# Difference attention's first round: which engine makes two low weight parts, and where two ternary means are summed

## The chip, the cores and the metric

The kernel runs on one core of one Trainium2 chip. The metric is the time of one execution on the device, in microseconds (us); lower is better. The core has five engines that run their own instruction streams and wait for each other through semaphores: TensorE (PE), VectorE (DVE), ScalarE (ACT), GpSimd (POOL) and SyncE (SP, which only issues transfers here).

## The reference

Two layers work on 8 x 64 tokens of width 512. Each is a cross attention, a self attention and a feed-forward block, each with a residual sum. The change lies in layer 0's self attention ("difference attention"), which computes, for 16 heads of width 128 split into two halves:

```python
x = layernorm(x)
q, k, v = x @ Wq, x @ Wk, x @ Wv                    # 512 x 2048 each
a1 = softmax(q[..., :64] @ k[..., :64].T / 8 + causal)
a2 = softmax(q[..., 64:] @ k[..., 64:].T / 8 + causal)
x = x + ((a1 - sigmoid(lambda_init) * a2) @ v) @ Wo
```

(The listing is a shortened form; the names are the reference's.) Beside it the kernel prepares the weights of the feed-forward block that follows. That block's weights are made ternary in groups of 64:

```python
scale = clip(mean(abs(w_g)), 1e-8)
w_hat = clip(round(w_g / scale), -1, 1) * scale
```

## The kernel before, in words

**Numbers.** Products of float32 are made of three fast matmuls (`mm3`, L41 to L43): every operand is split into a high part (rounded to the fp32r type) and a low part (the rest). Weights come by DMA into one of four buffers `w_raw` of 128 x 1024. ScalarE writes the high part (`split_high`, L153); the low part, raw minus high, is written either by GpSimd (`split_low`, L157) or by VectorE (`low`, L1689). Buffer 0 holds a piece of Wq, 1 of Wk, 2 of Wv, 3 of Wo. A buffer is refilled when its low part is done: `fill` waits on `split_lo[k]` in SP's queue.

**Rounds.** `DiffAttention` goes over `PAIRS` = 8 rounds `i`, two heads in each. In a round TensorE makes queries and keys, the scores (L1813), the values, then transposes the probabilities (L1836), multiplies them with the values (L1844), and one round later multiplies the result with W_o in `project(i - 1)`, which sums in PSUM banks 4 to 7 from round 1 to the end. ScalarE copies what TensorE leaves in banks 0 to 3 out of PSUM. VectorE does the softmax.

**The norm ahead of it.** The residual's last two 128-token tiles (m = 2, 3) are added by VectorE (L1207), their statistics taken (L193), the variance prepared (L262, a 128 x 2 operation), ScalarE takes the root (L267), VectorE normalises (`da_xn`, L275), TensorE transposes (L292), ScalarE writes the high part (`da_xT_high`, L286) and VectorE the low part (L280). The first two tiles went the same way some 7 us earlier.

**Ternary steps.** `TernaryWeights` has 24 steps `s` of 1024 columns, three to a round. A step is a load (`tw_raw`), on ScalarE a cast (`scalar_cast`, L2012), absolute values (L2016), signs (L2020) and a copy of the means out of PSUM (`scalar_wide`, L2024), on TensorE two matmuls that make the means (L2060), and on VectorE six operations (`vector_quantise`, L2040 to L2051). In every round steps 3i+2, 3i+3 and 3i+4 put their means in banks 0 and 1, which the values used before, one step after the other: each waits until the banks have been read.

**Order.** All queues are written out by hand. GpSimd's: `split_low(0)`, `split_low(2)` (`gpsimd_first`), then the end of the window attention, two memsets of `da_a` (L1553), a wait for the four tiles of `da_xn`, `split_low(1)`, `split_low(3)`. SP's, after the window attention: the mask, lambda, then `load(1, 0)`, `load(1, 1)`, `load(1, 2)` (L149), the ternary loads of steps 4 and 5 (L1997), `load(2, 0)`, step 6, `load(2, 1)`, `load(2, 2)`, `load(1, 3)`, steps 7 and 8, and so on. VectorE's in round 0: step 0's quantising, three small operations on lambda, `low(0)` for round 1, step 1's quantising, the softmax, `low(1)` and `low(2)` for round 1, step 2's quantising; from round 1 on `low(3)` stands at the end of a round.

Of the kernel before, what the change touches and what calls it, by code (L numbers as in the profile page):

```python
# [23 lines left out]
M = N // P  # L24
# [8 lines left out]
PAIRS = H // 2  # L33
# [139 lines left out]
class LayerNorm:  # L173
# [44 lines left out]
    def scalar(self, act):  # L218
        self.scalar_std(act)
        self.scalar_turned(act)  # L220
# [75 lines left out]
class ContextSums:  # L296
# [62 lines left out]
    def gpsimd(self, pool):  # L359
        nc = self.c.nc  # L360
        nc.gpsimd.memset(self.ones8[:, :], 1.0).then_inc(self.memsets, 1)
        nc.gpsimd.memset(self.col[:, :, 1], 1.0 / T).then_inc(self.memsets, 1)
        nc.gpsimd.memset(self.col[:, :, 2:32], 0.0).then_inc(self.memsets, 1)
# [1109 lines left out]
class DiffAttention:  # L1473
# [67 lines left out]
            if i < PAIRS - 1:  # L1541
                self.load(sp, i + 1, 3)

    FIRST = (0, 2)

    def gpsimd_first(self, pool):
        for k in self.FIRST:
            self.c.split_low(pool, k, self.f[k] + 1)

    def gpsimd(self, pool):  # L1550
        nc = self.c.nc
        for h in range(2):
            nc.gpsimd.memset(self.a[h][:, :, :], 0.0).then_inc(self.zero, 1)  # L1553
        pool.wait_ge(self.c.ln_xn, M * (self.ln.u + 1))
        for k in (1, 3):
            self.c.split_low(pool, k, self.f[k] + 1)

    def scalar_first(self, act):
        c, tw = self.c, self.tw
# [13 lines left out]
    def scalar(self, act):  # L1573
        c, nc, tw = self.c, self.c.nc, self.tw
        self.ln.scalar_half(act, 1)
        c.split_high(act, 1, self.f[1] + 1)
        for m in (2, 3):
            self.ln.scalar_high(act, m)
        tw.scalar_sign(act, 0)
        act.wait_ge(self.in_, 32)  # L1580
        nc.scalar.activation(self.lam[:, 1, :], self.lam[:, 0, :], ACT.Exp, scale=-1.0).then_inc(self.lam_e, 1)
        c.split_high(act, 3, self.f[3] + 1)

        def out_high(i):
            for h in range(2):
                act.wait_ge(self.o_done, 2 * i + h + 1)
                nc.scalar.copy(self.oh[h][:, :], c.bank[:, 2 + h, :]).then_inc(self.o_hi, 1)

        def queries(i, h):
            act.wait_ge(self.proj, 8 * i + h + 1)  # L1590
            if i:
                act.wait_ge(self.s_done, i)
            nc.scalar.copy(self.q[:, h, :], c.bank[:, h, :]).then_inc(self.q_out, 1)

        def keys(i, h):
            act.wait_ge(self.proj, 8 * i + h + 3)
            if i:
                act.wait_ge(self.s_done, i)
            nc.scalar.copy(self.k[:, h, :], c.bank[:, h, :]).then_inc(self.k_out, 1)

        def values(i, m):
            act.wait_ge(self.proj, 8 * i + 5 + m)
            if i:
                act.wait_ge(self.o_done, 2 * i)
            nc.scalar.copy(self.v[:, m, :], c.bank[:, m % 2, 0:2 * HD]).then_inc(self.v_out, 1)

        def exponentials(i, h):
            act.wait_ge(self.s_sub, 2 * i + h + 1)
            nc.scalar.activation(self.s[h][:, :, :], self.s[h][:, :, :], ACT.Exp).then_inc(self.e_done, 1)

        def probabilities(i, h):
            act.wait_ge(self.at_done, 2 * i + h + 1)
            nc.scalar.copy(self.at[h][:, :, :], c.bank[:, 2 + h, :].rearrange("p (m q) -> p m q", m=M)).then_inc(self.at_out, 1)

        for i in range(PAIRS):
            last = i == PAIRS - 1
            if i:
                out_high(i - 1)
            if i == 0:
                tw.scalar_sign(act, 1)  # L1620
                queries(0, 0)
                tw.scalar_cast(act, 2)
                tw.scalar_abs(act, 2)
                queries(0, 1)
                c.split_high(act, 0, self.f[0] + 2)
                tw.scalar_cast(act, 3)
                keys(0, 0)
                tw.scalar_abs(act, 3)
                keys(0, 1)
                tw.scalar_cast(act, 4)  # L1630
            else:
                tw.scalar_cast(act, 3 * i + 2)
                tw.scalar_abs(act, 3 * i + 2)
                queries(i, 0)
                if not last:
                    tw.scalar_cast(act, 3 * i + 3)
                queries(i, 1)
                if not last:
                    c.split_high(act, 0, self.f[0] + 2 + i)
                    tw.scalar_abs(act, 3 * i + 3)  # L1640
                keys(i, 0)
                if not last:
                    tw.scalar_cast(act, 3 * i + 4)
                    tw.scalar_abs(act, 3 * i + 4)
                keys(i, 1)
            if not last:
                act.wait_ge(self.proj, 8 * i + 4)
                c.split_high(act, 1, self.f[1] + 2 + i)
            values(i, 0)
            values(i, 1)  # L1650
            if i == 0:
                tw.scalar_abs(act, 4)
            exponentials(i, 0)
            values(i, 2)
            exponentials(i, 1)
            values(i, 3)
            tw.scalar_wide(act, 3 * i + 2, 0)
            tw.scalar_sign(act, 3 * i + 2)
            if not last:
                c.split_high(act, 2, self.f[2] + 2 + i)  # L1660
                tw.scalar_sign(act, 3 * i + 3)
                tw.scalar_wide(act, 3 * i + 3, 0)
            for h in range(2):
                probabilities(i, h)
            if not last:
                tw.scalar_wide(act, 3 * i + 4, 0)
            if i:
                act.wait_ge(self.y_done, M * i)
                c.split_high(act, 3, self.f[3] + 1 + i)
            if not last:  # L1670
                tw.scalar_sign(act, 3 * i + 4)
        out_high(PAIRS - 1)

    def vector(self, dve, ch, following):
        c, nc, tw = self.c, self.c.nc, self.tw
# [11 lines left out]
        def low(k, n):  # L1687
            dve.wait_ge(c.split_hi[k], n)
            v.tensor_tensor(c.wl[k][:, :], c.raw[k][:, :], c.wh[k][:, :].bitcast(F32), ALU.subtract).then_inc(c.split_lo[k], 1)  # L1689

        def out_low(i):
            for h in range(2):
                dve.wait_ge(self.o_hi, 2 * i + h + 1)
                v.tensor_tensor(self.ol[h][:, :], c.bank[:, 2 + h, :], self.oh[h][:, :].bitcast(F32), ALU.subtract).then_inc(self.o_lo, 1)
# [31 lines left out]
        for i in range(PAIRS):  # L1726
            last = i == PAIRS - 1
            if i:
                out_low(i - 1)
            if i:  # L1730
                tw.vector_quantise(dve, ch, 3 * i)
            if not last:
                low(0, self.f[0] + 2 + i)
            tw.vector_quantise(dve, ch, 3 * i + 1)
            softmax(i)
            if not last:
                low(1, self.f[1] + 2 + i)
                low(2, self.f[2] + 2 + i)
            tw.vector_quantise(dve, ch, 3 * i + 2)
            if i:  # L1740
                low(3, self.f[3] + 1 + i)
        out_low(PAIRS - 1)
        dve.wait_ge(tw.q_ok, tw.STEPS)
        for m in range(M):
# [30 lines left out]
    def tensor(self, pe):  # L1775
        c, nc, tw = self.c, self.c.nc, self.tw
        w = self.halves

        def project(i):
            pe.wait_ge(self.o_lo, 2 * i + 2)  # L1780
            pe.wait_ge(c.split_lo[3], self.f[3] + 1 + i)
            for m in range(M):
                for h in range(2):
                    o = tuple(t[h][:, m * P:(m + 1) * P] for t in (self.oh, self.ol))
                    ins = mm3(nc, c.bank[:, 4 + m, :], o, tuple(t[:, h * D:(h + 1) * D] for t in (c.wh[3], c.wl[3])),
                              i == 0 and h == 0, i == PAIRS - 1 and h == 1)
                ins.then_inc(self.y_done, 1)

        for i in range(PAIRS):
# [27 lines left out]
            for m in range(M):  # L1817
# [5 lines left out]
                    x = tuple(t[:, j, m * P:(m + 1) * P] for t in (self.to.xTh, self.to.xTl))  # L1823
                    ins = mm3(nc, c.bank[:, m % 2, 0:2 * HD], x, (wh[:, j, :], wl[:, j, :]), j == 0, j == C - 1)
                ins.then_inc(self.proj, 1)
            pe.wait_ge(self.v_out, 4 * i + 4)
            tw.tensor(pe, 3 * i + 2, 0)
            if i:
                project(i - 1)
            if i < PAIRS - 1:  # L1830
                pe.wait_ge(tw.wide_ok, 3 * i + 3)
                tw.tensor(pe, 3 * i + 3, 0)
            for h in range(2):
# [1 line left out]
                for m in range(M):  # L1835
                    ins = nc.tensor.transpose(c.bank[:, 2 + h, m * P:(m + 1) * P], self.a[h][:, m, :], c.ident[:, :])  # L1836
                ins.then_inc(self.at_done, 1)
            if i < PAIRS - 1:
                pe.wait_ge(tw.wide_ok, 3 * i + 4)
                tw.tensor(pe, 3 * i + 4, 0)  # L1840
            for h in range(2):
# [1019 lines left out]
class HadamardFFN:  # L2861
# [143 lines left out]
    def low(self, dve, t):  # L3005
        dve.wait_ge(self.w_hi, t + 1)
        self.c.nc.vector.tensor_tensor(self.l_w[t % 2][:, :], self.raw[t % self.RING], self.h_w[t % 2][:, :].bitcast(F32), ALU.subtract).then_inc(self.w_lo, 1)
# [343 lines left out]
```

## Time and profile before

| | |
|---|---|
| median of 3 runs | 884.65 us (881.57 to 886.21) |
| the profiled execution | 886.28 us |
| its span, first to last instruction | 884.4 us |
| TensorE busy | 804.7 us, 91% |
| VectorE busy | 619.1 us, 70% |
| ScalarE busy | 489.7 us, 55% |
| GpSimd busy | 170.3 us, 19% |
| mean granted TensorE clock | 0.969 of full speed |

All times inside the kernel are microseconds from the start of the span. The end of the window attention lies near 299 us, round 0 of difference attention reaches to about 335 us, and rounds 1 to 7 follow. "Busy" is an average over stages with different limits. A row of a timeline gives start, duration, engine, line, operation, the tile written and the tiles read; in square brackets stands how long the engine had been idle and what released it.

### The profile page before, as it was taken

The page shows a single profiled execution, that of the slowest core. Times are in us where ns is not written, and L with a number is a line of the kernel's source. Part 1 is how long each engine was busy: PE and PEld are TensorE (multiplying, and loading weights), DVE is VectorE, ACT ScalarE, POOL GpSimd, SP SyncE. Part 2 cuts the span into 40 slices and gives each one's busy share as a digit, 9 for nine tenths or more (in the row PEclk, how much of TensorE's full clock was granted, in tenths as well). Part 3 has the DMA queues.
Part 4 walks back from the last instruction along what each step waited for, and adds up shares of the span by engine and source line. Part 5 has one row for each costly group of instructions (what it writes and reads, how often), then busy time and mean ns, then how long its engine had stood idle before and what let it go on. Part 6 is the DMA issues. An engine that isn't in the chain of part 4 may idle for free.

```text
span 884.4 us, 13999 instructions
## 1 busy us (share of the span) xinstructions
PE 804.7 (91%) x5321; PEld 615.3 (70%) x5335; DVE 619.1 (70%) x1070; ACT 489.7 (55%) x818; POOL 170.3 (19%) x168
## 2 busy tenths in 40 slices
PE   3999999999799889999999998999977659999996
PEld 3897555677688668787878887534763537888885
DVE  6774876567866799999999987337798796333333
ACT  3565884223566687876787743445656635343431
POOL 3146540000155310000000000233122230211112
PEclk9999999999899889999999998999999978999999
DMA  8733566861123535434453005032024061212101
GB/s 310 259 109 123 187 216 215 290 235 55 60 90 125 170 123 167 145 97 127 134 165 97 27 25 162 32 118 96 25 79 164 28 223 64 72 49 72 47 1 47
DMA packets 49867, 106.80 MB, mean 121 GB/s; under 512 B 6714, under 2 KB 26098, under 8 KB 46220
## 3 DMA queue, kind: packets, MB, share of 16 engines
q1 hardware_dynamic: 48908, 95.33, 32.5%
q0 software_dynamic: 896, 10.62, 3.1%
q8 instruction: 41, 0.67, 0.3%
q14 instruction: 22, 0.18, 0.1%
HBM read 100.69 MB, written 5.25 MB: 120 GB/s over the span
## 4 chain that ended last, share of the span: by engine, by line
PE 79%; DVE 13%; ACT 5%; issue 2%; DMA 1%; SPq 0%; POOL 0%; ACTq 0%; DVEq 0%
PE banks L41 16%; PE banks L43 15%; PE banks L42 15%; PE banks L2277 6%; PE banks L412 3%; PE banks L1388 2%; PE banks L2307 2%; PE banks L1844 2%; PE banks L2308 2%; PE banks L1249 1%; PE banks L1418 1%; PE banks L2108 1%; PE banks L1391 1%; PE banks L2060 1%; PE banks L1269 1%
## 5 line engine op out<-in xcount | busy, mean ns | idle before, releaser
L157 POOL TENSOR_TENSOR w_low<-w_raw,w_high 128x256 fp32r<-128x256 f32 (+2 forms) x44 | 58.4, 1335 | 152.8 <-ACT w_high L153 151.0
L153 ACT CAST w_high<-w_raw 128x1024 fp32r<-128x1024 f32 (+2 forms) x74 | 56.8, 779 | 22.7 <-PE banks L43 22.5
L41 PE MATMUL banks<-da_xT_high,w_high 128*128 128x512 f32 (+1 forms) x136 | 53.0, 390 | 1.7 <-DVE da_xT_low L280 1.7
L41 PE MATMUL banks<-hf_xhh,w_high 128*128 128x512 f32 (+1 forms) x136 | 51.8, 381 | 0.6 <-DVE hf_xhl L3031 0.6
L43 PE MATMUL banks<-da_xT_high,w_low 128*128 128x512 f32 (+1 forms) x136 | 52.2, 384 | 0.0
L42 PE MATMUL banks<-da_xT_low,w_high 128*128 128x512 f32 (+1 forms) x136 | 52.0, 382 | 0.0
L43 PE MATMUL banks<-hf_xhh,w_low 128*128 128x512 f32 (+1 forms) x136 | 51.9, 381 | 0.0
L42 PE MATMUL banks<-hf_xhl,w_high 128*128 128x512 f32 (+1 forms) x136 | 51.7, 380 | 0.0
L2947 POOL TENSOR_TENSOR hf_hl<-hf_h,hf_hh 128x512 fp32r<-128x512 f32 x16 | 24.3, 1520 | 123.2 <-ACT hf_hh L3003 123.2
L3011 DVE TENSOR_TENSOR hf_downW_l<-dw_w,hf_downW_h 128x512 fp32r<-128x512 f32 x16 | 11.2, 699 | 50.7 <-ACT hf_downW_h L2963 50.7
L2277 PE MATMUL banks<-ff_xT_high,tw_guT 128*128 128x512 f16 x120 | 45.5, 380 | 0.0
L2277 PE MATMUL banks<-ff_xT_low,tw_guT 128*128 128x512 f16 x120 | 45.5, 379 | 0.0
L2157 POOL MEMSET ff_acc<- 128x512 f32 x1 | 0.5, 524 | 233.1 <-DVE x_res L1746 233.1
L1689 DVE TENSOR_TENSOR w_low<-w_raw,w_high 128x1024 fp32r<-128x1024 f32 x28 | 33.7, 1224 | 7.5 <-ACT w_high L153 7.3
L41 PE MATMUL banks<-w_high,da_xT_high 128*128 128x256 f32 x128 | 36.5, 285 | 0.0
L42 PE MATMUL banks<-w_low,da_xT_high 128*128 128x256 f32 x128 | 35.6, 278 | 0.0
L43 PE MATMUL banks<-w_high,da_xT_low 128*128 128x256 f32 x128 | 35.6, 278 | 0.0
L3060 DVE TENSOR_TENSOR hf_downH_l<-banks,hf_downH_h 128x512 fp32r<-128x512 f32 x16 | 11.1, 691 | 34.8 <-ACT hf_downH_h L2999 34.8
L2993 ACT ACTIVATE hf_silu<-banks,hf_scales 128x512 f32<-128x512 f32 x16 | 11.0, 688 | 43.2 <-PE banks L43 43.0
L2024 ACT CAST tw_wide<-banks 128x1024 bf16<-128x1024 f32 x24 | 24.5, 1020 | 18.3 <-PE banks L2060 18.3
L963 ACT COPY wa_cn<-banks 72x512 f32<-72x512 f32 x16 | 9.3, 581 | 43.2 <-PE banks L1399 43.2
L2225 DVE TENSOR_TENSOR ff_e<-ff_e,banks 128x512 f32<-128x512 f32 x16 | 11.0, 686 | 29.9 <-PE banks L2277 26.7
(443 smaller groups left out, 2487.9 us busy)
## 6 DMA issues: line engine op xcount, KB each, us to landing
cs_rows<-in_ctx SPq DMA_DIRECT2D x24, 1024.0 KB, 5.1
tw_raw<-in_L_ffn_w_gate_up SPq DMA_DIRECT2D x16, 512.0 KB, 4.5
hf_raw<-in_L_ffn_W_up SPq DMA_DIRECT2D x16, 512.0 KB, 3.5
w_raw<-in_L_xattn_W_o SPq DMA_DIRECT2D x8, 512.0 KB
w_raw<-in_L_attn_Wq SPq DMA_DIRECT2D x8, 512.0 KB
w_raw<-in_L_attn_Wk SPq DMA_DIRECT2D x8, 512.0 KB
w_raw<-in_L_attn_Wv SPq DMA_DIRECT2D x8, 512.0 KB
w_raw<-in_L_attn_Wo SPq DMA_DIRECT2D x8, 512.0 KB
```

The costliest lines, as they stand in the source:

```text
L41: nc.tensor.matmul(out, a[0], b[0], start=start, stop=False)
L42: nc.tensor.matmul(out, a[0], b[1], start=False, stop=False)
L43: return nc.tensor.matmul(out, a[1], b[0], start=False, stop=stop)
L153: self.nc.scalar.copy(self.wh[k][:, 0:cols], self.raw[k][:, 0:cols]).then_inc(self.split_hi[k], 1)
L157: self.nc.gpsimd.tensor_tensor(self.wl[k][:, 0:cols], self.raw[k][:, 0:cols], self.wh[k][:, 0:cols].bitcast(F32), ALU.subtract).then_inc(s ...
L412: ins = nc.tensor.matmul(c.bank[32 * r:32 * r + 32, bank, :], self.col[:, k * self.R4 + r, :], self.rows[k][:, r, :], start=(k == 0), stop ...
L1388: nc.tensor.matmul(out[a], queries(self.qa, 8 * g), keys(self.kvcT[:, g // 16, g % 16, :, :]), start=True, stop=False)
L1689: v.tensor_tensor(c.wl[k][:, :], c.raw[k][:, :], c.wh[k][:, :].bitcast(F32), ALU.subtract).then_inc(c.split_lo[k], 1)
L1844: ins = nc.tensor.matmul(c.bank[:, 2 + h, m * P:(m + 1) * P], self.v[:, m, h * HD:(h + 1) * HD], self.at[h][:, m, :], start=True, stop=True)
L2024: self.c.nc.scalar.copy(self.wide[s % self.DEEP][:, :].rearrange("p (a n) -> p a n", a=2), self.c.bank[:, bank:bank + 2, :]).then_inc(self ...
L2277: ins = nc.tensor.matmul(c.bank[:, 2 * k + n, :], w.guT[:, bass.ds(i * 2 + k, 1), n, j, :].rearrange("p a q -> p (a q)"), part[:, j, :], s ...
L2947: g.tensor_tensor(self.hp[1][t % 2][:, :], self.h[t % 2][:, :], self.hp[0][t % 2][:, :].bitcast(F32), ALU.subtract).then_inc(self.hl_ok, 1)
```

## The change

GpSimd no longer makes the low parts of Wv (buffer 2) and Wo (buffer 3) for round 0. VectorE makes them: the one of Wv after the lambda operations and ahead of `low(0)`, the one of Wo at the end of round 0. `split_low(0)` and `split_low(1)` stay on GpSimd. In round 0, the means of steps 2 and 3 go to banks 4, 5 and 6, 7, side by side, without a wait for the values' copies or for each other; step 4's go to banks 0 and 1 after all four values have been copied, no longer after step 3's copy. From round 1 on nothing is changed.

```diff
     def gpsimd_first(self, pool):
-        for k in self.FIRST:                      # FIRST = (0, 2)
-            self.c.split_low(pool, k, self.f[k] + 1)
+        self.c.split_low(pool, 0, self.f[0] + 1)
...
         pool.wait_ge(self.c.ln_xn, M * (self.ln.u + 1))
-        for k in (1, 3):
-            self.c.split_low(pool, k, self.f[k] + 1)
+        self.c.split_low(pool, 1, self.f[1] + 1)
...
-            tw.scalar_wide(act, 3 * i + 2, 0)
+            tw.scalar_wide(act, 3 * i + 2, 0 if i else 4)
...
-                tw.scalar_wide(act, 3 * i + 3, 0)
+                tw.scalar_wide(act, 3 * i + 3, 0 if i else 6)
...
+            if i == 0:
+                low(2, self.f[2] + 1)
             if not last:
                 low(0, self.f[0] + 2 + i)
...
-            if i:
-                low(3, self.f[3] + 1 + i)
+            low(3, self.f[3] + 1 + i)
...
-            pe.wait_ge(self.v_out, 4 * i + 4)
-            tw.tensor(pe, 3 * i + 2, 0)
-            if i:
+            if i == 0:
+                for s in (2, 3):
+                    tw.tensor(pe, s, 2 * s)
+            else:
+                pe.wait_ge(self.v_out, 4 * i + 4)
+                tw.tensor(pe, 3 * i + 2, 0)
                 project(i - 1)
-            if i < PAIRS - 1:
+            if 0 < i < PAIRS - 1:
                 pe.wait_ge(tw.wide_ok, 3 * i + 3)
                 tw.tensor(pe, 3 * i + 3, 0)
...
-            if i < PAIRS - 1:
+            if i == 0:
+                pe.wait_ge(self.v_out, M)
+                tw.tensor(pe, 4, 0)
+            elif i < PAIRS - 1:
                 pe.wait_ge(tw.wide_ok, 3 * i + 4)
                 tw.tensor(pe, 3 * i + 4, 0)
```

## Rows read from the trace of the kernel before

**Rows 1.** The page's chain that ended last: its shares by engine.

```profile
PE 79%; DVE 13%; ACT 5%; issue 2%; DMA 1%; SPq 0%; POOL 0%; ACTq 0%; DVEq 0%
```

**Rows 2.** The same chain in order of time: start us, us, what.

```profile
300.33 2.74 DVE ln_std L262
...
306.85 0.96 ACT tw_sg L2020
...
331.20 0.85 PE banks L2060 x2
332.05 3.13 PE banks L1844 x16
...
390.98 1.93 PE banks L1844 x16
```

**Rows 3.** Timeline of VectorE, 292 to 338 us.

```profile
292.81 0.17 DVE L262 TENSOR_SCALAR ln_std<-ln_mean_var 128x2 f32<-128x2 f32 x1
...
298.53 0.69 DVE L1207 TENSOR_TENSOR x_res<-x_res,banks 128x512 f32<-128x512 f32 x1
...
310.84 2.78 DVE L2051 TENSOR_TENSOR tw_guT<-tw_w,tw_abs 128x1024 bf16<-128x1024 bf16 x1
...
315.29 1.23 DVE L1689 TENSOR_TENSOR w_low<-w_raw,w_high 128x1024 fp32r<-128x1024 f32 x1 [1.08 <-ACT w_high L153]
...
319.79 0.69 DVE L2051 TENSOR_TENSOR tw_guT<-tw_w,tw_abs 128x1024 bf16<-128x1024 bf16 x1
...
324.37 0.68 DVE L1712 TENSOR_REDUCE da_r<-da_s 128x8 f32<-128x512 f32 x1
...
336.30 1.28 DVE L1694 TENSOR_TENSOR da_ol<-banks,da_oh 128x512 fp32r<-128x512 f32 x2
```

**Rows 4.** Timeline of GpSimd, 299 to 314 us.

```profile
299.71 2.40 POOL L157 TENSOR_TENSOR w_low<-w_raw,w_high 128x1024 fp32r<-128x1024 f32 x1 [8.11 <-ACT w_high L153]
302.04 0.99 POOL L1553 MEMSET da_a<- 128x512 f32 x2
304.68 2.35 POOL L157 TENSOR_TENSOR w_low<-w_raw,w_high 128x1024 fp32r<-128x1024 f32 x1 [1.64 <-DVE da_xn L275]
310.34 2.74 POOL L157 TENSOR_TENSOR w_low<-w_raw,w_high 128x1024 fp32r<-128x1024 f32 x1 [3.32 <-ACT w_high L153]
```

**Rows 5.** Timeline of TensorE: both halves of the norm's transposes, the probabilities' second transposes.

```profile
296.06 1.03 PE L292 MATMUL banks<-ident,da_xn 128*128 128x128 f32 x8
...
304.29 1.94 PE L292 MATMUL banks<-ident,da_xn 128*128 128x128 f32 x8 [2.47 <-DVE da_xn L275]
...
330.08 1.12 PE L1836 MATMUL banks<-ident,da_a 128*128 128x128 f32 x4 [1.78 <-DVE da_a L1724]
```

**Rows 6.** Timeline of ScalarE, 296 to 345 us.

```profile
296.70 1.07 ACT L286 CAST da_xT_high<-banks 128x512 fp32r<-128x512 f32 x2 [1.64 <-PE banks L292]
...
318.17 1.05 ACT L2012 CAST tw_w<-tw_raw 128x1024 bf16<-128x1024 f32 x1
...
322.09 0.37 ACT L1605 COPY da_v<-banks 128x256 f32<-128x256 f32 x1 [0.99 <-PE banks L43]
...
323.32 0.63 ACT L1609 ACTIVATE da_s<-da_s 128x512 f32<-128x512 f32 x1
...
343.96 1.05 ACT L2012 CAST tw_w<-tw_raw 128x1024 bf16<-128x1024 f32 x1
```

**Rows 7.** Timeline of SP's queue: steps 4 and 5, `load(1, 3)`, steps 7 and 8.

```profile
312.67 3.80 SPq L1997 DMA_DIRECT2D tw_raw<-in_L_ffn_w_gate_up  x2
...
332.89 0.50 SPq L149 DMA_DIRECT2D w_raw<-in_L_attn_Wo  x1
336.78 3.11 SPq L1997 DMA_DIRECT2D tw_raw<-in_L_ffn_w_gate_up  x2
```

**Rows 8.** The seven `tw_raw` loads issued between 285 and 345 us.

```profile
DMA to landing us min/median/max: 3.6/4.2/8.7
```

**Rows 9.** Windows of 1 us: PE, PEld, DVE, ACT, POOL busy, granted clock, DMA share, GB/s.

```profile
331.00:332.00 1.00, 1.00 (x4) 0.64 (x3) 1.00 (x2) 0.82 (x2) 0.00 (x0) 0.50 0.00 0
```

More of the change, by code:

```diff
@@ L1542, in sync @@
                 self.load(sp, i + 1, 3)
-    FIRST = (0, 2)
     def gpsimd_first(self, pool):
-        for k in self.FIRST:
-            self.c.split_low(pool, k, self.f[k] + 1)
+        self.c.split_low(pool, 0, self.f[0] + 1)
     def gpsimd(self, pool):
```

## The prediction, made before the changed kernel was run

> **What bounds the kernel now.** I read the page's chain first: TensorE holds 79% of the path that sets the end [rows 1], so work of another engine counts only where TensorE waits. Then I followed the chain in order of time from the end of the window attention to round 1. There, between 299 and 330 us, it leaves TensorE: the norm's second half on VectorE, then ScalarE from 306.85 us, then VectorE's `low(0)`, quantising and softmax, and it returns to TensorE at 330.08 [rows 2, 5]. From there on each round is a closed row of matmuls, so a gain made before 330 us is carried to the end if nothing new waits. The third view was each engine's timeline in this stretch, to see what lay beside the slow pieces.
>
> Two VectorE rows stand out. L262, an operation on 128 x 2 numbers, takes 0.17 us for the first two tiles and 2.73 us for the last two: it starts at 300.33 and ends at 303.07 [rows 2, 3]. GpSimd's `split_low(2)` runs from 299.71 to 302.11 and its memsets to 303.03 [rows 4]. L2051 takes 2.78 us where the next one takes 0.69; it ends 0.5 us after `split_low(3)`, which lasts from 310.34 to 313.08 [rows 3, 4]. So VectorE stands still while GpSimd works.
>
> The Trainium skill, "SBUF — State Buffer", section "Who interferes with whom", says that an operation in a two-port mode, or one with two SBUF inputs against a reading GpSimd operation, blocks wholly until the other has ended. By it both stalls are GpSimd's, which the two rows' ends agree with, and the new VectorE operations with two SBUF inputs would be blocked as well wherever GpSimd still reads; it does not after 304.5 us in the schedule below.
>
> **`split_low(2)` leaves GpSimd.** GpSimd then goes straight to the memsets, which wait for the residual's last sum, done at 298.53 + 0.69 = 299.22; 0.99 us of memsets end at 300.2, just before L262's 300.33 [rows 3, 4]. L262 falls to 0.17: gain 2.56 us. Bounds: if the memsets stand in front of it for their whole length, 2.56 - 0.99 = 1.57; nothing speaks for more than 2.56. I take 2.56, since they have 0.1 us to spare.
>
> **TensorE's clock at the transposes.** TensorE waited 2.47 us for `da_xn` and did the second half's eight transposes in 1.94 us; the first half, without a wait, took 1.03 [rows 5]. With L262 short they start at 304.29 - 2.56 = 301.73, when TensorE, free at 304.29 - 2.47 = 301.82, has only just ended the queries. They should run at the higher clock. From the first transpose to the end of both copies it was 306.85 - 304.29 = 2.56 us [rows 2, 5] and in the first half 296.70 + 1.07 - 296.06 = 1.71 [rows 5, 6]: gain 0.85 at most, 0 at least. I take 0.85, and leave out the 0.1 that TensorE may start late: with the 2.56, **3.4 us**.
>
> **ScalarE's stretch** begins 3.4 us sooner and keeps its order; it loses no operation there.
>
> **`low(2)` for round 0 on VectorE**, 1.23 us [rows 3]. It stands before `low(0)`, where VectorE idled 1.08 us for ScalarE. The stall on L2051, 2.78 - 0.69 = 2.09, goes too, with `split_low(3)`. So VectorE had 1.08 + 2.09 = 3.17 us of room there, and uses 1.23. Against it, `split_low(1)` is released by `da_xn` and gains only 2.56: it ends at 304.68 + 2.35 - 2.56 = 304.47, while step 0's quantising would begin at 304.1; 0.3 us more, covered. Left over: 1.6 us. Cost 0; without the cover 1.23. What is late next is ScalarE's high part, as now. The values' weights are then ready near 310.3; TensorE reads them only behind the keys and the scores, and `low(0)`, which comes after them here, not before 315.29 - 3.4 = 311.9.
>
> **`low(3)` for round 0**, 1.23 us, at the round's end. Behind it wait the low parts of the attention output, step 3's quantising and round 1's softmax. From round 1 on the same operation stands in the same place, and the rounds stay closed rows of matmuls, so VectorE has room for it; I cost it at 0, upper bound 1.23. `project(0)` reads it behind round 1's queries, keys and values.
>
> **Means in banks 4 to 7.** TensorE makes them right behind the values instead of after two waits. But it then waits 1.78 us for the probabilities, a VectorE result [rows 5]; being earlier only lengthens that wait. ScalarE's copies and signs keep their order and end, as now, before it can take up the second transposes. Gain 0, cost 0. The order is also legal for the residual's banks, since W_o's sums begin a round later.
>
> **SP's queue.** `load(1, 2)` now waits for VectorE, and steps 4 and 5 stand behind it. L2051 ends at 313.62 - 2.09 - 3.4 + 0.3 = 308.4, lambda takes 0.6, `low(2)` 1.23: 310.3; with 0.5 us of issuing, step 4's load goes out at 310.8 instead of 312.67 [rows 3, 7]. ScalarE casts it at 318.17 - 3.4 = 314.8 [rows 6]. At the median landing of 4.2 us [rows 8] it is there at 315.0, 0.2 late. Behind that cast ScalarE has 0.99 us idle, and the exponentials end at 323.95 while VectorE takes them up at 324.45, 0.5 later [rows 3, 6]: 1.5 us of cover. Cost 0. Likewise `load(1, 3)` waits for `low(3)`, at 336.30 - 3.4 + 1.23 = 334.1 (332.89 now [rows 7]), and step 7's load goes at 334.7, is cast at 343.96 - 3.4 = 340.6 [rows 6]: 5.9 us for a landing of 4.2. Cost 0.
>
> **Sum.** 2.56 + 0.85 = 3.4, everything else 0. The profiled execution took 886.28 us for a span of 884.4, and would take 882.9 with a span of 881.0; the median of the runs is 1.6 lower, and 884.65 - 3.4 = **881.3 us**, 0.4% less. About 0.5% (4.4 us) is what a measurement of this kernel can tell from no change, so by that bound this is "the same".
>
> **Rivals.**
> (a) *The clock stays high at 330 us.* Now the granted clock is 0.50 there [rows 9], and transposes, means and L1844 take 1.12 + 0.85 + 3.13 us [rows 2, 5]. At the higher level L1844 takes 1.93, the others half: 1.2 + 1.0 = 2.2 us more, 879.1. For it: TensorE has two more matmuls behind the values. Against it: its waits for the two heads' probabilities come out longer, so it is less busy, not more. The Trainium skill, "TensorE: Matmul & The Clock Gate", Part 1, says that the gate follows how busy the engine was; that would leave the clock low here.
> (b) *Only a part:* the memsets take 0.99, or the transposes stay slow. 1.6 to 2.6 us gained, 882 to 883.
> (c) *L262's length is not GpSimd's*, or another operation takes up the stall: no gain, 884.7. The two coinciding ends speak against it.
> (d) *Slower: SP's held-back loads land late.* With a landing time L, step 4's cast costs L - 5.5 (310.8 + L, less 314.8 and 1.5), step 7's L - 5.9, and the latter sits ahead of a key copy that TensorE waits for. At L = 8.7, the slowest row, these are 3.2 and 2.8: 6.0 - 3.4 = 2.6 us slower, 887.3. It decides from L = 7.4. Against it: the slow landing stood behind four loads; here one load is ahead.
>
> **Chances.** Forecast 0.52, (a) 0.16, (b) 0.15, (c) 0.09, (d) 0.08. The range 878.0 to 885.6 goes from (a) with 1 us of the runs' own spread below it to (c) with 1 above it, leaving out (d) and the outer tails. The likeliest case alone is 880 to 882.6. Over 0.5% faster needs more than 4.4 us: (a) mostly, and a fifth to a quarter of the forecast's spread, 0.28. Over 0.5% slower, (d) at its worst, 0.04. The rest 0.68.
>
> **What the profile after would show.** L262 at 0.2 us near 300.3; transposes of 1.0 us at 301.8; L2051 at 0.69 everywhere; `low(2)` ending near 310.3, no new ScalarE wait for `tw_raw`; second transposes of the probabilities at 326.7; round 1 3.4 us earlier and the offset constant to the end. Wrong would be the forecast if the memsets move into L262, if ScalarE idles before L2012, or if the clock's low stretches move.

## The result and the profile after

The changed kernel takes 882.15 us in the median of 22 runs (880.20 to 883.26), the kernel before 884.73 us (22 runs, 881.01 to 886.99). The ratio is 0.997, 95% interval 0.9961 to 0.9979: 1.9 to 3.5 us faster by it. The forecast was 881.3 us within 878.0 to 885.6. By the bound of 0.5% this counts as the same; by its interval it is a small gain. The profiled execution's span fell from 884.4 to 880.4 us.

The same operations carry line numbers here that differ by a few: the memsets are L1550, `low` is L1685, the ternary cast L2015, the quantising ends at L2054, and the product with the values is L1847 instead of L1844. First VectorE, for comparison with [rows 3]:

```profile
298.83 0.69 DVE L1207 TENSOR_TENSOR x_res<-x_res,banks 128x512 f32<-128x512 f32 x1
...
300.63 0.17 DVE L262 TENSOR_SCALAR ln_std<-ln_mean_var 128x2 f32<-128x2 f32 x1
...
304.52 0.54 DVE L2043 TENSOR_SCALAR tw_wide<-tw_wide 128x1024 bf16<-128x1024 bf16 x1
...
308.00 0.69 DVE L2054 TENSOR_TENSOR tw_guT<-tw_w,tw_abs 128x1024 bf16<-128x1024 bf16 x1
...
309.30 1.22 DVE L1685 TENSOR_TENSOR w_low<-w_raw,w_high 128x1024 fp32r<-128x1024 f32 x1
312.10 1.23 DVE L1685 TENSOR_TENSOR w_low<-w_raw,w_high 128x1024 fp32r<-128x1024 f32 x1 [1.57 <-ACT w_high L153]
```

L262 is down to 0.17 us, L2054 to 0.69, and after `low(2)` VectorE still waits 1.57 us for ScalarE; 1.6 was forecast. GpSimd, against [rows 4]:

```profile
299.58 1.00 POOL L1550 MEMSET da_a<- 128x512 f32 x2 [7.70 <-DVE x_res L1207]
302.42 2.36 POOL L157 TENSOR_TENSOR w_low<-w_raw,w_high 128x1024 fp32r<-128x1024 f32 x1 [1.83 <-DVE da_xn L275]
```

The memsets end at 300.58, 0.05 us ahead of L262. TensorE, against [rows 5]:

```profile
302.03 1.06 PE L292 MATMUL banks<-ident,da_xn 128*128 128x128 f32 x8
...
326.89 1.12 PE L1836 MATMUL banks<-ident,da_a 128*128 128x128 f32 x4 [2.19 <-DVE da_a L1720]
```

The transposes take 1.06 instead of 1.94 us and begin without a wait. The granted clock beside them, first before, then after (it is the sixth value behind the window's length):

```profile
304.30:306.20 1.90, 1.90 (x8) 1.52 (x8) 0.47 (x2) 0.59 (x1) 1.52 (x1) 0.50 0.00 0
```

```profile
302.00:303.00 1.00, 1.00 (x9) 0.85 (x8) 0.34 (x1) 0.35 (x2) 0.58 (x1) 1.00 0.61 172
```

From the first transpose to the end of both copies it was 2.56 us before [rows 2, 5] and is 302.69 + 1.07 - 302.03 = 1.73 us now. The probabilities' second transposes start 326.89 - 298.83 = 28.06 us after the start of the residual's last sum (L1207). Before it was 330.08 - 298.53 = 31.55 [rows 3, 5]. The difference, **3.49 us**, is the forecast's sum of 3.4. This measure leaves out what comes before and after; it is used below as "the distance". It is read from one execution of each kernel. ScalarE and SP's queue:

```profile
315.28 1.05 ACT L2015 CAST tw_w<-tw_raw 128x1024 bf16<-128x1024 f32 x1 [0.16 <-DMA tw_raw<-in_L_ffn_w_gate_up]
```

```profile
310.56 0.39 SPq L149 DMA_DIRECT2D w_raw<-in_L_attn_Wv  x1
310.99 2.40 SPq L2000 DMA_DIRECT2D tw_raw<-in_L_ffn_w_gate_up  x2
...
334.36 0.39 SPq L149 DMA_DIRECT2D w_raw<-in_L_attn_Wo  x1
334.79 2.31 SPq L2000 DMA_DIRECT2D tw_raw<-in_L_ffn_w_gate_up  x2
```

Step 4's load was held back and ScalarE waited 0.16 us for it, covered; step 7's was no hindrance.

Not all of the 3.49 us arrives. The chain after, from the probabilities to round 1's second key copy:

```profile
326.89 1.12 PE banks L1836 x4
328.01 0.85 PE banks L2063 x2
328.86 3.41 PE banks L1847 x16
...
343.44 0.59 ACT da_k L1595
```

And before, where 331.20 and 332.05 stand in [rows 2], the copy:

```profile
346.23 0.59 ACT da_k L1599
```

From transposes to copy are 16.55 us, before 16.15, so 0.4 us went back: the low clock ended 4.7 us behind the start of these transposes before (at 334.8) and 5.6 us behind it after (at 332.5). Whether that belongs to the change is open. In both traces the low stretch lasted 6.9 us; in Wo alone and banks alone, the next experiments, it was only half as long. The largest difference after that is again one of the clock. Windows near the end of round 7, first before, then after:

```profile
540.00:542.00 2.00, 2.00 (x6) 1.63 (x5) 1.25 (x2) 0.00 (x0) 0.00 (x0) 0.50 1.01 343
```

```profile
540.00:542.00 2.00, 2.00 (x16) 1.73 (x16) 1.86 (x3) 0.00 (x0) 0.70 (x3) 1.00 0.00 0
```

The granted clock is 0.50 against 1.00. (The counts, six matmuls against sixteen, are not of the same work: the last W_o product ended at 540.4 in the changed kernel and at 545.4 before.) That product took 7.36 us before and 5.73 after. The changed kernel's own low stretch came later, from 544.0 to 547.5 us; the kernel before had a second one too, from 549.7 to 553.3. So the 4.0 us between the two spans are one execution against one: 3.49 at the distance, less 0.40 up to the key copy, plus 1.21 behind it, less 0.30 by which the changed kernel's execution was late already at L1207. The number for the change is the difference of the medians, 2.6 us.

### The profile page after: what moved, and what is told of

Its sections match the earlier page's. It is cut to its first block, busy times and chain, and to the rows that moved or that the text cites. A ratio compares the mean times of both kernels' runs of the same rounds, so it can differ in the third digit from the quotient of the medians.

```text
span 880.4 us, 13997 instructions
## 1 busy us (share of the span) xinstructions
PE 804.1 (91%) x5321; PEld 615.0 (70%) x5335; DVE 616.8 (70%) x1072; ACT 489.7 (56%) x818; POOL 164.9 (19%) x166
## 4 chain that ended last, share of the span: by engine, by line
PE 79%; DVE 11%; ACT 6%; issue 2%; DMA 1%; SPq 0%; POOL 0%; ACTq 0%; DVEq 0%
PE banks L41 16%; PE banks L43 15%; PE banks L42 15%; PE banks L2280 6%; PE banks L412 2%; PE banks L1388 2%; PE banks L1847 2%; PE banks L2310 2%; PE banks L2311 2%; PE banks L1418 1%; PE banks L1249 1%; PE banks L2111 1%; PE banks L1391 1%; PE banks L2063 1%; PE banks L1269 1%
## 5 line engine op out<-in xcount | busy, mean ns | idle before, releaser
L157 POOL TENSOR_TENSOR w_low<-w_raw,w_high 128x256 fp32r<-128x256 f32 (+2 forms) x42 | 53.2, 1275 | 141.3 <-ACT w_high L153 139.3
L1685 DVE TENSOR_TENSOR w_low<-w_raw,w_high 128x1024 fp32r<-128x1024 f32 x30 | 36.1, 1223 | 6.7 <-ACT w_high L153 6.4
```

Source lines behind the costliest of these rows:

```text
L157: self.nc.gpsimd.tensor_tensor(self.wl[k][:, 0:cols], self.raw[k][:, 0:cols], self.wh[k][:, 0:cols].bitcast(F32), ALU.subtract).then_inc(s ...
```

## The experiments

All times are medians, of 10 to 12 runs in the first seven rows that give one and of 5 or 6 in the others; intervals are those of the ratio to the kernel before, on the same chip. "Distance" and, in the last column, the time from the same start to round 1's second key copy are those of one profiled execution each. The changed kernel was measured twice more against the kernel before: it came out 3.5 us faster ("changed, again") and 5.0 us faster ("changed, control"), beside the 2.6 of the result.

| kernel | median us | ratio (95%) | distance us | to the key copy us |
|---|---|---|---|---|
| before | | | 31.55 | 47.70 |
| changed | | | 28.06 | 44.61 |
| Wv alone | 880.28 | 0.9953 (0.9927 to 0.9980) | 29.43 | 46.10 |
| Wo alone | 884.75 | 0.9994 (0.9975 to 1.0014) | 31.55 | 47.48 |
| banks alone | 884.66 | 0.9989 (0.9968 to 1.0010) | 31.56 | 47.10 |
| changed, again | 881.15 | 0.9957 (0.9936 to 0.9979) | 28.08 | 44.73 |
| Wv on GpSimd behind the norm | 882.88 | 0.9982 (0.9972 to 0.9991) | 29.42 | 45.16 |
| changed, six memsets | 881.72 | 0.9966 (0.9950 to 0.9982) | 28.95 | 44.67 |
| before, matmuls at the transposes | 883.45 | 0.9989 (0.9975 to 1.0003) | 30.04 | 45.61 |
| changed, matmuls at the probabilities | 879.84 | 0.9943 (0.9925 to 0.9961) | 28.08 | 42.81 |
| changed, control | 880.22 | 0.9944 (0.9931 to 0.9957) | 28.08 | 44.51 |
| the same with matmuls, again | 879.30 | 0.9944 (0.9925 to 0.9963) | 28.07 | 42.81 |
| matmuls in both places | 877.85 | 0.9925 (0.9911 to 0.9939) | 28.06 | 42.80 |
| Wv alone, step 4's load ahead | 880.50 | 0.9949 (0.9936 to 0.9962) | 28.47 | 44.68 |

### The three parts by themselves

Wv alone:

```diff
-    FIRST = (0, 2)
+    FIRST = (0,)
...
+            if i == 0:
+                low(2, self.f[2] + 1)
             if not last:
                 low(0, self.f[0] + 2 + i)
```

> Alone: the low part of round 0's Wv goes from GpSimd to VectorE; Wo's stays on GpSimd, the means stay in banks 0 and 1. Theory (GpSimd's reading operation stands in front of L262): L262 at 0.2 us near 300.5, round 1 some 3 us earlier, the whole 2 to 3.4 us faster, as the full change. The stall beside Wo's low part stays on whatever VectorE runs at that time, and costs nothing as long as VectorE still reaches low(0) before ScalarE has its high part. Rival (the banks or Wo do the work): under 1 us faster.

The time says faster by 0.2 to 0.7%, 4.4 us in the medians. The distance is 29.43: 2.1 us nearer instead of 3.5. So in this trace, though not in the time, one sentence of the expectation was wrong: the stall beside Wo's part does cost something. ScalarE, VectorE and SP in this kernel:

```profile
315.20 1.05 ACT L2014 CAST tw_w<-tw_raw 128x1024 bf16<-128x1024 f32 x1 [3.36 <-DMA tw_raw<-in_L_ffn_w_gate_up]
```

```profile
304.71 2.75 DVE L2053 TENSOR_TENSOR tw_guT<-tw_w,tw_abs 128x1024 bf16<-128x1024 bf16 x1
...
308.09 2.36 DVE L1689 TENSOR_TENSOR w_low<-w_raw,w_high 128x1024 fp32r<-128x1024 f32 x2
...
319.25 0.69 DVE L1712 TENSOR_REDUCE da_r<-da_s 128x8 f32<-128x512 f32 x1 [0.87 <-ACT da_s L1609]
```

```profile
309.34 0.39 SPq L149 DMA_DIRECT2D w_raw<-in_L_attn_Wv  x1
309.77 0.96 SPq L1999 DMA_DIRECT2D tw_raw<-in_L_ffn_w_gate_up  x2
```

L2053 (the last operation of the quantising) stands 2.1 us longer, `low(2)` is late, and SP stands behind it. Step 4's load goes out at 309.77, counted from L1207 2.1 us later than in the changed kernel, and lands 5.4 us later. ScalarE waits 3.36 us for it, and of these 0.87 reach VectorE's softmax. The rest of the lost 1.4, 0.5 us, is mostly VectorE ending `low(0)` 0.4 us late, since both low parts now stand in one piece behind the stall (the last experiment parts the two). That is rival (d) in small, mostly from a late issue and in part from a slower landing: where ScalarE waited for this load in a trace of the changed kernel it had landed after 4.3 to 5.2 us. With a landing of 4.3 the wait would have been 1.1 us shorter and, by an estimate from these rows, nothing of it would have reached the softmax.

Wo alone:

```diff
-        for k in (1, 3):
-            self.c.split_low(pool, k, self.f[k] + 1)
+        self.c.split_low(pool, 1, self.f[1] + 1)
...
-            if i:
-                low(3, self.f[3] + 1 + i)
+            low(3, self.f[3] + 1 + i)
```

> Alone: the low part of round 0's Wo goes to VectorE at the end of the round. Theory: L2051 falls from 2.8 to 0.7 us, VectorE only waits longer for ScalarE in front of low(0), L262 stays at 2.7, time unchanged within 1 us. Rival (VectorE bounds this stretch): up to 2.1 us faster.

No change in the time, the distance the same 31.55. L262 stays long, L2049 is short, and VectorE only waits 3.2 us for ScalarE:

```profile
300.65 2.72 DVE L262 TENSOR_SCALAR ln_std<-ln_mean_var 128x2 f32<-128x2 f32 x1
...
311.15 0.69 DVE L2049 TENSOR_TENSOR tw_guT<-tw_w,tw_abs 128x1024 bf16<-128x1024 bf16 x1
```

Banks alone: the hunks on `scalar_wide` and on TensorE's means, with nothing moved off GpSimd.

> Alone: round 0's means of steps 2 and 3 in banks 4 to 7. Theory: TensorE only waits longer for the probabilities; second transposes at the same distance from the norm, time unchanged within 1 us. Rival (TensorE's waits for the banks count): about 1 to 2 us faster. If TensorE's clock profits from the two matmuls that follow the values directly, up to 2.2 us faster.

No change in the time; distance 31.56. TensorE waits longer for the same probabilities, 2.20 us instead of 1.78. The low clock behind that wait lasted half as long as before (330.1 to 333.6), but so it did in Wo alone (331.5 to 335.0), where the banks are as before, so this is not shown to be the banks' doing.

The changed kernel beside them:

> The changed kernel as it is, beside the three parts on one chip. Expected: ratio 0.997, 2 to 3.5 us faster, equal to Wv alone within 1 us.

3.5 us faster in the medians, distance 28.08. Wv alone is at 880.28 and the whole change at 881.15 (the means are 880.9 for both), so the expected equality within 1 us came true: the 1.4 us that the traces show between the two do not show in the time.

### Where the reading operation stands in time

Wv's part stays on GpSimd, but behind the norm:

```diff
-    FIRST = (0, 2)
+    FIRST = (0,)
...
-        for k in (1, 3):
+        for k in (1, 2, 3):
             self.c.split_low(pool, k, self.f[k] + 1)
```

> The kernel before with one move: Wv's low part stays on GpSimd but stands behind the wait for the norm, after Wk's. Theory (it is where the reading operation stands in time, not who makes it): L262 at 0.2 us, and GpSimd's operation now stands in front of step 0's quantising on VectorE for some 2.4 us, which VectorE's room before low(0) covers only in part with the stall beside Wo's part still there: 1.5 to 3.4 us faster. Rival (work moved off GpSimd is what counts, or VectorE has no room): under 1 us faster.

The ratio is 0.9982, 0.8 to 2.5 us faster by the interval; the distance is 29.42. L262 takes 0.17. GpSimd now works from 301.73 to 309.42 in one piece, and two operations of step 0 stand still, for GpSimd's second and third:

```profile
301.73 7.69 POOL L157 TENSOR_TENSOR w_low<-w_raw,w_high 128x1024 fp32r<-128x1024 f32 x3 [1.84 <-DVE da_xn L275]
```

```profile
304.40 2.78 DVE L2042 TENSOR_TENSOR tw_abs<-tw_abs,tw_wide 128x1024 bf16<-128x1024 bf16 x1
307.21 2.75 DVE L2044 TENSOR_TENSOR tw_abs<-tw_abs,tw_wide 128x1024 bf16<-128x1024 bf16 x1
310.00 0.69 DVE L2047 TENSOR_TENSOR tw_abs<-tw_abs,tw_sg 128x1024 bf16<-128x1024 bf16 x1
...
312.76 1.22 DVE L1689 TENSOR_TENSOR w_low<-w_raw,w_high 128x1024 fp32r<-128x1024 f32 x1
```

`low(0)` no longer waits for ScalarE: VectorE sets the pace here. So for L262 it is the place in time that counts and not which engine makes the part, and VectorE's room is smaller than two such stalls.

### Memsets over the norm

```diff
-        for h in range(2):
-            nc.gpsimd.memset(self.a[h][:, :, :], 0.0).then_inc(self.zero, 1)
+        for t in (*self.a, *self.at, *self.s):
+            nc.gpsimd.memset(t[:, :, :], 0.0).then_inc(self.zero, 1)
...
-        dve.wait_ge(self.zero, 2)
+        dve.wait_ge(self.zero, 6)
```

> The changed kernel with six memsets of 128 x 512 instead of two (a further two each on da_at and da_s, which are overwritten later), some 3 us from 299.6 to 302.6, over L262 and the normalising L275. If a writing GpSimd operation holds up VectorE's tensor_scalar for its whole length and the next one goes ahead too, L262 ends only near 302.6 and 1.5 to 2.3 us of the gain go. If VectorE gets in between two memsets, L262 takes 0.2 to 0.7 us and L275 some more, costing 0.5 to 1.5 us. If memsets don't stand in the way, no change from the changed kernel.

The distance grows from 28.06 to 28.95, by 0.9. In the time (881.72) this can't be told, and at round 1's second key copy it is gone (44.67 us against 44.51 to 44.73): the low clock behind the probabilities lasted only 3.5 us in this execution (329.1 to 332.6). The middle expectation came true: VectorE gets in between memsets. L262 takes 0.43 instead of 0.17 us and the two L275 take 1.60 instead of 1.00.

```profile
300.75 0.43 DVE L262 TENSOR_SCALAR ln_std<-ln_mean_var 128x2 f32<-128x2 f32 x1
...
301.72 1.60 DVE L275 TENSOR_SCALAR da_xn<-x_res,ln_mean_var,ln_std 128x512 f32<-128x512 f32 x2
```

### TensorE's clock

Matmuls in the kernel before, in the wait for `da_xn`:

```diff
         pe.wait_ge(self.tw.wide_ok, 2)
+        for _ in range(9):
+            c.nc.tensor.matmul(c.bank[:, 2, :], wh[:, 0, 0:P], c.wh[0][:, 0:512], start=True, stop=True)
         for m in (2, 3):
             self.ln.tensor_quarter(pe, m)
```

> The kernel before with nine matmuls of 512 columns into bank 2 (overwritten by the transposes) in the 2.5 us in which TensorE waits for da_xn. It tells the clock's term from the stall's. Theory: the second half's eight transposes take 1.0 instead of 1.9 us, the rest of the chain stands as before: 0.6 to 0.9 us faster, at the edge of what can be told. Rival (the transposes' slowness is not the idling's): 1.9 us again and no change.

The ratio's interval includes 1; the distance is 30.04, 1.5 us nearer. The transposes take 1.03 us, as the theory has it. But two other things happened. L262 took 1.80 instead of 2.73: here VectorE came in between GpSimd's subtraction (298.30 + 2.39 = 300.69) and the memsets. And the transposes began 0.96 us after the start of L275, before 0.70: the nine matmuls were somewhat too many, and up to 0.13 of these 0.26 us is L275 itself, which took 1.13 beside the memsets. From the first transpose to the end of both copies it was 302.85 + 1.07 - 302.21 = 1.71 us instead of 2.56, the 0.85 of the forecast. 0.93 + 0.85 - 0.26 = 1.52 is the gain in distance. The granted clock was 1.00 at these transposes and 0.50 before, so the clock's term is shown, though not in the time.

```profile
298.92 1.80 DVE L262 TENSOR_SCALAR ln_std<-ln_mean_var 128x2 f32<-128x2 f32 x1
...
301.25 1.13 DVE L275 TENSOR_SCALAR da_xn<-x_res,ln_mean_var,ln_std 128x512 f32<-128x512 f32 x2
```

```profile
300.15 2.23 PE L1770 MATMUL banks<-w_high 128*128 128x512 f32 x9
302.21 1.03 PE L292 MATMUL banks<-ident,da_xn 128*128 128x128 f32 x8
```

Matmuls in the changed kernel, in both waits for the probabilities:

```diff
             for h in range(2):
+                if i == 0:
+                    pe.wait_ge(self.v_out, M)
+                    for _ in range((6, 8)[h]):
+                        nc.tensor.matmul(c.bank[:, 0, :], self.to.xTh[:, 0, 0:P], self.to.xTh[:, 0, :], start=True, stop=True)
                 pe.wait_ge(self.a_done, 4 * i + 2 * h + 2)
```

> The changed kernel with six and eight matmuls of 512 columns into bank 0 (overwritten by step 4's means) in the two waits of round 0 for the probabilities. By the price of the clock in rival (a): granted clock 1.0 from 326 to 332 us instead of 0.5; second transposes, step 4's means and L1847 fall from 5.4 to some 2.9 us: 2 to 2.5 us faster than the changed kernel, 4.5 to 6 us faster than the kernel before. Rival (ScalarE's copies of the probabilities or the new matmuls themselves bound that piece): under 1 us.

879.84 us, 4.8 below its kernel before. The same kernel again, now beside a control:

> The changed kernel again, as control for the next three on the same chip: 2 to 3.5 us faster than the kernel before.

> The changed kernel with fourteen matmuls in round 0's two waits for the probabilities, again, now beside its control. Clock's theory: 1.5 to 2.5 us faster than the control. Rival (the first comparison was the spread between chips): within 0.7 us of the control.

The control was 5.0 us faster than the kernel before (3.8 to 6.1 by the interval), more than was expected. It gave 880.22, the kernel with the matmuls 879.30: 0.9 us in the medians, with overlapping intervals, between what the theory and the rival expected. But its six runs fall into two groups: 877.81, 877.82 and 877.94 us with a mean granted clock of 0.977 or 0.978, and 880.65, 881.47 and 882.32 with 0.972 to 0.974, where the control's five runs (879.64 to 882.25) have 0.968 to 0.973. So in half of its runs the time shows no gain. (Of the six runs of the first comparison five have 0.979 or 0.980, and all six of the next experiment 0.977 to 0.980.) The trace is of the first group:

```profile
325.01 0.66 PE L1840 MATMUL banks<-ident,da_a 128*128 128x128 f32 x4 [0.36 <-DVE da_a L1720]
325.51 0.59 PE L2067 MATMUL banks<-tw_abs,tw_mean 128*128 128x512 bf16 x2
325.94 1.95 PE L1851 MATMUL banks<-da_at,da_v 128*128 128x128 f32 x16
```

```profile
326.00:328.00 2.00, 2.00 (x19) 1.95 (x18) 1.97 (x4) 2.00 (x3) 0.00 (x0) 1.00 0.31 86
```

```profile
336.18 0.59 ACT L1595 COPY da_k<-banks 128x512 f32<-128x512 f32 x1 [0.26 <-PE banks L43]
337.71 1.05 ACT L2019 CAST tw_w<-tw_raw 128x1024 bf16<-128x1024 f32 x1 [0.94 <-DVE tw_guT L2058]
...
339.75 0.57 ACT L1595 COPY da_k<-banks 128x512 f32<-128x512 f32 x1
```

L1851 takes 1.95 us where L1847 took 3.62, the clock is 1.00 where the changed kernel's was 0.50, and the distance of 28.07 shows that nothing was held back. From transposes to key copy are now 14.74 us, against 16.55 in the changed kernel's first trace, 16.65 in its second and 342.93 - 326.50 = 16.43 in the control's: 1.7 to 1.9 us. Rival (a) priced it at 2.2, and at the first key copy it is that and more: 336.18 - 325.01 = 11.17 us against 340.18 - 326.50 = 13.68 in the control, 2.5 us. Then 0.8 us are lost again, because ScalarE's cast ahead of the second key copy waits 0.94 us for step 3's quantising (L2058). VectorE works without a pause from the low parts at 324.99 us up to it, and 1.22 us of that row are `low(3)`, which the change put there. So VectorE's room for `low(3)` is used up as soon as TensorE runs this stretch at the higher clock. That the wait would be gone without `low(3)` is an estimate from these rows; no run tests it.

A further seven in front of the last W_o product:

```diff
+        pe.wait_ge(tw.wide_ok, 3 * PAIRS)
+        for _ in range(7):
+            nc.tensor.matmul(c.bank[:, 0, :], self.to.xTh[:, 0, 0:P], self.to.xTh[:, 0, :], start=True, stop=True)
         project(PAIRS - 1)
```

> The same with seven more matmuls into bank 0 in front of the last W_o product, where TensorE waits 1.8 us for VectorE. In the kernel before the granted clock was 0.5 from 539.7 to 542.8 behind that wait, in the changed kernel's trace it was not. If this stretch is slow in some executions only: 0 to 1 us faster than without these seven in the median. If the seven matmuls hold back the product: up to 0.5 us slower.

877.85 us, ratio 0.9925 (0.9911 to 0.9939): the fastest here, 2.4 us below the control in the medians. The intervals overlap, but the runs themselves hardly do (877.21 to 879.66 against 879.64 to 882.25). TensorE still waits 0.23 us behind the seven matmuls, so they delayed nothing:

```profile
531.12 0.50 PE L41 MATMUL banks<-w_high,da_oh 128*128 128x512 f32 x1 [0.23 <-DVE da_ol L1690]
```

Against the fourteen alone it is 1.45 us, with six runs of each, more than the 0 to 1 expected. The traces show no part of it: the last W_o product takes 5.7 us with and without the seven, and the next low stretch is 541.2 to 544.7 us with them and 541.3 to 544.8 without. The difference in the medians comes from the fourteen alone having three runs above 880 us and this kernel none; whether the seven prevent such runs is not settled.

### The held-back load

Wv alone as above, and step 4's load ahead of the Wv load:

```diff
-        for k in range(3):
+        for k in range(2):
             self.load(sp, 1, k)
...
                 tw.load(sp, 3 * i + 4)
+            if i == 0:
+                self.load(sp, 1, 2)
+            if i < PAIRS - 1:
                 tw.load(sp, 3 * i + 5)
```

> Wv's part alone on VectorE (as in the first experiment), with step 4's load ahead of the Wv load in SP's queue. In the first experiment ScalarE waited 3.4 us for step 4's load, since Wo's part on GpSimd held VectorE's L2051 for 2.1 us ahead of low(2), and SP stood behind low(2); the second transposes came 2.1 us nearer to the residual's last sum than before instead of 3.5. Theory (the wait is SP's order alone): no ScalarE wait for tw_raw, 3.4 to 3.5 us nearer. Rival (low(2) being late itself counts): 2.1 us as before.

ScalarE no longer waits for a load; the distance is 28.47, 1.0 us nearer than with Wv alone and 0.4 short of the changed kernel. In these traces both sides held a part: 1.0 us is SP's order (with the slow landing of the first experiment in it), and the other 0.4 is VectorE itself, which reaches `low(0)` without a wait, both low parts in one piece:

```profile
309.60 2.36 DVE L1692 TENSOR_TENSOR w_low<-w_raw,w_high 128x1024 fp32r<-128x1024 f32 x2
```

At the second key copy nothing of the 0.4 is left (44.68 us, the changed kernel 44.51 to 44.73), and the median of 880.50 is 0.3 above the control's.

## Why the prediction was right, by its steps

- **`split_low(2)` leaves GpSimd, 2.56 us.** Right: L262 fell from 2.73 to 0.17, and the memsets were done before it, by 0.05 us rather than 0.1. Wv alone and the move behind the norm show both that this is the cause. Taken too simply was what the operation waits for: the forecast's sum holds with the 2.73 of one trace. In another execution with the same order on GpSimd it was 1.80. So the loss here was between 1.6 and 2.6 us in the traces, and the gain varies with it.
- **The clock at the transposes, 0.85.** Right in the trace: 1.06 instead of 1.94 us at a granted clock of 1.00 instead of 0.50, and 1.73 instead of 2.56 us to the end of the copies, 0.83. Together with the 2.56, 3.41 was forecast, and the distance fell by 3.49.
- **`low(2)` at 0.** Right, 1.57 us of wait left. **The stall on L2051 at 0.** By itself (Wo alone) its removal is worth nothing. Beside the Wv move the traces show it at up to 1.4 us of distance, since without it `low(2)` is late and SP stands behind it; 0.4 of that is VectorE's lateness, and up to 1.0 hangs on how fast one load landed. In the time the kernel without it was no slower (880.28 against 881.15 us). The forecast had this chain of causes only as rival (d).
- **`low(3)` at 0, banks at 0.** Right at the clock that the changed kernel has there: Wo alone and banks alone leave the distance at 31.55 and 31.56. With matmuls that keep the clock up, VectorE's row with `low(3)` in it costs 0.8 us behind the first key copy, so the room that the forecast found there by analogy with later rounds depends on TensorE's low clock.
- **SP's queue at 0.** Right: 0.16 us late where 0.2 was worked out. In the control the same wait was 1.09 us, and the distance 28.08 all the same, within the 1.5 us of cover.
- **The sum, 3.4 of 884.65.** Three comparisons of the same two kernels gave 2.6, 3.5 and 5.0 us, with intervals of 1.9 to 3.5, 1.9 to 5.7 and 3.8 to 6.1. The first and the last exclude each other, so the spread from one comparison to the next is larger than the intervals say, and the forecast's 3.4 lies inside that spread. How near the median of 882.15 came to 881.3 is therefore in part luck; the trace confirms the terms better than the time can. Two things move the gain in single executions: how long L262 is before, and where the low clock behind the probabilities ends (0.4 us between the first two traces).
- **Rivals.** (a) did not come by itself: the granted clock was 0.50 again. With extra matmuls it could be had, 2.5 us at the first key copy, of which 1.7 to 1.9 are left at the second. (b) did not come in its mechanism, L262 took 0.17 us and the transposes 1.06, but its band of 882 to 883 us holds the measured 882.15, so the time alone could not have told it from the forecast. (c) is refuted. (d) did not come; its chain of causes is real and was seen with Wv alone.

By the Trainium skill, "SBUF — State Buffer", section "Who interferes with whom", a VectorE operation with two SBUF inputs stands behind a GpSimd operation that reads and came first: the two of 2.78 and 2.75 us agree. L280, which reads one input from PSUM, ran at its usual 1.29 us for two beside GpSimd's subtraction (303.31 to 304.60 us in the changed kernel, the subtraction 302.42 to 304.78), as the same section has it for one SBUF input. L262 has one SBUF input too and was held all the same; the prediction's rule covers it only as an operation in a two-port mode, and that L262 runs in one is not shown by any run.

## What to carry to other kernels

Look for tiny VectorE operations with long durations on the chain, and for a GpSimd operation that ends just where they do. Here moving that one out of their time gave 2.56 us of the chain, and moving another one, beside an operation that had room, gave nothing by itself. Before a low part is moved to an engine that is busier, ask which transfers its semaphore lets go and who stands behind them in the queue: a load issued 2.1 us later could cost up to 1.0 us or nothing, by how it landed. Where a wait of a few microseconds can't be removed, idle matmuls into a free bank can keep TensorE's clock for what follows; then look again at the engines that had room only because TensorE was slow.

## What the hardware showed unexpectedly

L262 with the same order of work on GpSimd took 2.73, 2.72 and 2.72 us in three profiled executions and 1.80 in another. In the three it ended with the second memset (at 303.06 and 303.03 us in the kernel before), in the other with the subtraction (300.72 and 300.69): sometimes VectorE comes in between GpSimd's subtraction and its memset, sometimes only behind both memsets, and nothing in the rows ahead of it tells the two apart. With six memsets in a row, L262 took 0.26 us more and the two L275 together 0.6 us more, each no more than the rest of one memset of 0.5 us explains. And a wait of 1.09 us for a load in ScalarE's stretch left no trace in the distance (28.08), while one of 3.36 did. The granted clock behind the same wait for the probabilities was low for 6.9 us in some executions and for 3.5 in others (Wv alone 327.3 to 330.8), and with the matmuls in the wait not at all in three of three traces.
